# Graph layers: rows through DRAM lines and spreading loads, and score masks added by two DMAs a block

## The reference

```python
for l in range(3):
    si = x @ attn_w[l, :d]
    sj = x @ attn_w[l, d:]
    scores = si[:, :, None] + sj[:, None, :] + attn_b[l]
    scores = jnp.where(scores >= 0, scores, 0.2 * scores)
    scores = jnp.where(mask, scores, -jnp.inf)
    attn = jax.nn.softmax(scores, axis=-1)
    agg = jnp.einsum('bij,bjd->bid', attn, x)
    h = layernorm(x + agg, g1[l], beta1[l])
    ff = jax.nn.gelu(h @ W1[l] + b1[l], approximate=False) @ W2[l] + b2[l]
    x = layernorm(h + ff, g2[l], beta2[l])
```

## Time and profile before

| | |
|---|---|
| time, median of 3 runs | 2490.27 us (2487.1 to 2490.76) |
| the profiled execution's own time | 2482.05 us |
| its span in the trace | 2480.2 us |
| block with `v_row` (odd k), first two layers | 37.3 us |
| block without `v_row` (even k), first two layers | 36.3 us |
| ten blocks of the last layer (34 to 43) | 377.2 us |
| TensorE clock granted, mean of the execution | 0.974 |

### The profile page before, as it was taken

The page is one execution under the profiler, slowest core; times in us unless marked ns, Lnnn a source line. Parts: engine busy times, 40 slices in busy tenths (PEclk is TensorE's granted clock), DMA queues, the critical chain, the costliest instruction groups (busy, mean ns, idle before and its releaser), DMA issues. The chain is left out here.

```text
span 2480.2 us, 45887 instructions
## 1 busy us (share of the span) xinstructions
PE 2361.1 (95%) x16548; PEld 2187.9 (88%) x16548; DVE 2072.0 (84%) x4806; ACT 1784.7 (72%) x2849; POOL 1122.7 (45%) x1317
## 2 busy tenths in 40 slices
PE   7999999993599999999999999999999999999996
PEld 6999999982499999999999999999999999999996
DVE  5888888885678998988878898998887989889875
ACT  3444445442478888888878889888887888888883
POOL 3555555563233353453434353354443555544531
PEclk9999999996699999999999999999999999999998
DMA  4444444444646657755666757656666566566441
GB/s 149 136 139 139 145 146 139 143 124 111 176 117 151 175 138 174 182 144 144 156 169 163 168 143 179 169 138 158 162 160 166 147 162 158 140 170 133 116 110 43
DMA packets 382131, 364.78 MB, mean 147 GB/s; under 512 B 218064, under 2 KB 312272, under 8 KB 381904
## 3 DMA queue, kind: packets, MB, share of 16 engines
q1 hardware_dynamic: 354256, 261.17, 38.5%
q0 software_dynamic: 27648, 100.68, 17.3%
HBM read 152.07 MB, written 58.72 MB: 85 GB/s over the span
## 5 line engine op out<-in xcount | busy, mean ns | idle before, releaser
L1490 PE MATMUL A<-x_hi,pT_hi 128*128 128x258 f32 x1536 | 439.4, 286 | 28.5 <-DVE pT_lo L1233 21.7
L1144 ACT ACTIVATE g<-G,b_less 128x512 f32<-128x512 f32 x384 | 264.4, 688 | 261.7 <-PE G L45 260.1
L1491 PE MATMUL A<-x_hi,pT_lo 128*128 128x258 f32 x1536 | 437.1, 285 | 0.0
L1492 PE MATMUL A<-x_lo,pT_hi 128*128 128x256 f32 x1536 | 434.3, 283 | 0.0
L1541 PE MATMUL Y<-w,g_hi 128*128 128x256 f32 x1536 | 433.0, 282 | 0.0
L1542 PE MATMUL Y<-w,g_hi 128*128 128x256 f32 x1536 | 427.0, 278 | 0.0
L1543 PE MATMUL Y<-w,g_lo 128*128 128x256 f32 x1536 | 426.6, 278 | 0.0
L1049 POOL DMA_DIRECT2D t<-maskT x192 | 173.4, 955 | 403.6 <-DVE t L1226 398.5
L1233 DVE TENSOR_TENSOR pT_lo<-t,pT_hi 128x512 fp32r<-128x512 f32 x384 | 259.0, 687 | 103.7 <-ACT t L1109 103.4
L1322 DVE TENSOR_TENSOR g_lo<-g,g_hi 128x512 fp32r<-128x512 f32 x384 | 264.2, 688 | 93.5 <-ACT g_hi L1147 90.1
L1490 PEld LDWEIGHTS A<-x_hi,pT_hi 128*128 128x128 f32 x1536 | 293.2, 191 | 37.9 <-issue 22.6
(11 more groups left out here) (184 smaller groups left out, 6082.1 us busy)
## 6 DMA issues: line engine op xcount, KB each, us to landing
t<-maskT POOLq DMA_DIRECT2D x192, 512.0 KB, 4.7
mask<-mask SPq DMA_DIRECT2D x192, 256.0 KB, 2.9
a_adj_t<-in_adj SPq DMA_DIRECT2D x64, 512.0 KB, 4.0
x_rows<-rows SPq DMA_DIRECT2D x24, 1024.0 KB, 6.6
mask<-a_mask SPq DMA_DIRECT2D x64, 256.0 KB, 4.3
rows<-xo SPq DMA_DIRECT2D x32, 512.0 KB, 2.9
a_xs<-in_x SPq DMA_DIRECT2D x9, 1024.0 KB, 9.6
x_rows<-in_x SPq DMA_DIRECT2D x8, 1024.0 KB, 7.2
```

Of the source, the lines that this page charges most:

```text
L1490: pe.matmul(L.A[:, t, 0:DE], hi, L.x_hi[:, par, j, :], start=(j == 0), stop=False)
L1491: pe.matmul(L.A[:, t, 0:DE], lo, L.x_hi[:, par, j, :], start=False, stop=False)
L1492: mm = pe.matmul(L.A[:, t, 0:D], hi, L.x_lo[:, par, j, :], start=False, stop=(j == NT - 1))
```

## The change

1. **Rows.** For blocks 2 to 47 PE makes one small transpose per graph instead of the eight: `r_line` (rcol, 128 by 16, to 16 by 128) at f = 2 of even blocks, and `v_line` (vcol, 128 by 8, to 8 by 128) at f = 1 of odd blocks. ACT copies the result to a small SBUF tile, SP stores it as a line in DRAM, and SP loads that line back into all 128 partitions (`partition_broadcast`). 21 such lines for vrow, 23 for rrow; each rrow line is read by four loads of 256 KB, each vrow line by one of 512 KB. The first three v rows and the first two r rows are made as before.
2. **Masks.** `add_masks` issues two DMAs of four tiles (semaphores tm0 and tm1) in place of four of two. The first needs score tile 3 and now stands behind `deviation1`; the second needs score tile 7 and stands behind `deviation3`. `exps` of tiles 4 and 5 therefore now waits for the DMA that needs score tile 7.

```diff
@@ masks, SP and POOL
                 if k > 0:
-                    for g in range(2 * half, 2 * half + 2):
-                        sp.wait_ge(L.s_tm[g], 16 * k)
+                    sp.wait_ge(L.s_tm[half], 16 * k)
...
             def add_masks(k, groups):
                 for g in groups:
-                    pool.wait_ge(L.s_t, NT * k + 2 * g + 2)
-                    pool.wait_ge(L.s_maskT[g // 2], 16 * (k + 1))
-                    pool.dma_start(L.t[:, 2 * g:2 * g + 2, :], L.maskT[:, 2 * g:2 * g + 2, :], accum_op=ALU.add).then_inc(L.s_tm[g], 16)
+                    gs = slice(HALF * g, HALF * (g + 1))
+                    pool.wait_ge(L.s_t, NT * k + HALF * (g + 1))
+                    pool.wait_ge(L.s_maskT[g], 16 * (k + 1))
+                    pool.dma_start(L.t[:, gs, :], L.maskT[:, gs, :], accum_op=ALU.add).then_inc(L.s_tm[g], 16)
@@ ACT, exps
-                act.wait_ge(L.s_tm[j // 2], 16 * (k + 1))
+                act.wait_ge(L.s_tm[j // HALF], 16 * (k + 1))
@@ SP, rows
+            def store_v(n):
+                sp.wait_ge(L.s_vline, n - PB + 1)
+                sp.dma_start(vline[n].rearrange("(s p) -> s p", p=P), L.v_line[:, :]).then_inc(L.s_vline_out, 16)
+
+            def load_v(n):
+                sp.wait_ge(L.s_vline_out, 16 * (n - PB + 1))
+                sp.wait_ge(L.s_top, NT * (n - 1))
+                sp.dma_start(L.vrow[:, n % 2, :], vline[n].partition_broadcast(P)).then_inc(L.s_vrow_in[n % 2], 16)
...
+            def load_r(k):
+                n, cs = k // 2, slice(k % 2 * BANK, (k % 2 + 1) * BANK)
+                sp.wait_ge(L.s_rline_out, 16 * n)
+                sp.wait_ge(L.s_t, NT * (k - 1))
+                for part in range(2):
+                    sp.dma_start(L.rrow[:, part, k % 2, :], rline[n, part, cs].partition_broadcast(P)).then_inc(L.s_rrow_in[k % 2], 16)
@@ PE, rows
+            def v_line(n):
+
+                pe.wait_ge(L.s_vprep, 4 * n + 1)
+                pe.transpose(L.A[0:NT, 2, 0:P], L.vcol[:, :], L.ident[:, :]).then_inc(L.s_vlineT, 1)
+
+            def r_line(n):
+
+                pe.wait_ge(L.s_cols, COLS * (n + 1))
+                pe.transpose(L.A[0:2 * NT, 0, 0:P], L.rcol[:, :, :].rearrange("p a s -> p (a s)"), L.ident[:, :]).then_inc(L.s_rlineT, 1)
```

More of the change, by code:

```diff
@@ L732, in layer_buffers @@
     L.s_vrow = sem("vrow")
+    L.s_vlineT = sem("vlineT")
+    L.s_vline = sem("vline")
+    L.s_vline_out = sem("vline_out")
+    L.s_vrow_in = [sem(f"vrow_in{i}") for i in range(2)]
     L.s_top = sem("top")
@@ L736, in layer_buffers @@
     L.s_rrow = sem("rrow")
+    L.s_rlineT = sem("rlineT")
+    L.s_rline = sem("rline")
+    L.s_rline_out = sem("rline_out")
+    L.s_rrow_in = [sem(f"rrow_in{i}") for i in range(2)]
     L.s_t = sem("t")
-    L.s_tm = [sem(f"tm{i}") for i in range(4)]
+    L.s_tm = [sem(f"tm{i}") for i in range(2)]
     L.s_exp = sem("exp")
@@ L770, in layer_buffers, with graph_layers @@
     return L
-def graph_layers(nc, L, x, rows, out, mask, split, par):
+def graph_layers(nc, L, x, rows, out, mask, split, vline, rline, par):
     attn_w, attn_b, W1, b1, W2, b2, g1, be1, g2, be2 = par
@@ L927, in _ @@
                     load_x1(k - 2)
+                if k % 2 == 1 and k + 2 < K:
+                    load_r(k + 2)
                 for f in split_at(k):
@@ L942, in _ @@
                     load_maskT(k + 2, 0)
+                for n in r_made(k):
+                    store_r(n)
+                for n in v_made(k):
+                    if n >= PB:
+                        store_v(n)
                 for f in split_at(k):
@@ L947, in _ @@
                         load_split(arriving, f)
+                for n in v_made(k):
+                    if n >= PB:
+                        load_v(n)
+                for n in r_made(k):
+                    load_r(2 * n)
                 for r in tops[2:]:
@@ L1054, in _ @@
             v_prepare(1)
-            add_masks(0, range(4))
+            add_masks(0, range(2))
             for k in range(K + 2):
@@ L1061, in _ @@
                         row_columns((k + 2) // 2, part)
-                for n in rows_made(k):
+                for n in v_made(k):
                     v_prepare(n)
-                if k + 1 < K:
-                    add_masks(k + 1, range(1))
                 if k < K:
@@ L1068, in _ @@
                 if k + 1 < K:
-                    add_masks(k + 1, range(1, 3))
+                    add_masks(k + 1, range(1))
                 if k - 2 >= K - C:
@@ L1072, in _ @@
                 if k + 1 < K:
-                    add_masks(k + 1, range(3, 4))
+                    add_masks(k + 1, range(1, 2))
         @block.scalar
@@ L1089, in copy_v, with copy_v_line, copy_r_line @@
                 act.activation(L.vrow[:, n % 2, :].rearrange("p (c i) -> p c i", c=2), L.A[:, 2:4, :], ACT.Copy).then_inc(L.s_vrow, 1)
+            def copy_v_line(n):
+                act.wait_ge(L.s_vlineT, n - PB + 1)
+                if n > PB:
+                    act.wait_ge(L.s_vline_out, 16 * (n - PB))
+                act.activation(L.v_line[:, :], L.A[0:NT, 2, 0:P], ACT.Copy).then_inc(L.s_vline, 1)
+            def copy_r_line(n):
+                act.wait_ge(L.s_rlineT, n)
+                if n >= 2:
+                    act.wait_ge(L.s_rline_out, 16 * (n - 1))
+                act.activation(L.r_line[:, :], L.A[0:2 * NT, 0, 0:P], ACT.Copy).then_inc(L.s_rline, 1)
             def x_hi(j):
@@ L1184, in _ @@
                     if f == 3:
-                        for n in rows_made(k):
-                            copy_v(n)
-                    if f == 4 and k + 2 < K:
-                        for part in range(2):
-                            copy_rows(k + 2, part)
+                        for n in v_made(k):
+                            if n < PB:
+                                copy_v(n)
+                            else:
+                                copy_v_line(n)
+                        for n in r_made(k):
+                            copy_r_line(n)
                     if f in (5, 6) and k < K:
@@ L1568, in _ @@
                         pe.wait_ge(L.s_u, TC * (k + 1))
-                        for n in rows_made(k):
-                            v_row(n)
-                    if f == 2 and k + 2 < K:
-                        r_rows(k + 2)
+                        for n in v_made(k):
+                            if n < PB:
+                                v_row(n)
+                            else:
+                                v_line(n)
+                    if f == 2:
+                        for n in r_made(k):
+                            r_line(n)
                     if ffn:
@@ L1585, in program @@
     split = nc.dram_tensor("split", (layers - 1, W1.shape[2] // P, P, 4, D), F32, kind="Internal").ap()
+    vline = nc.dram_tensor("vline", (layers * B, N), F32, kind="Internal").ap()
+    rline = nc.dram_tensor("rline", (layers * B, 2, N), F32, kind="Internal").ap()
     chunks = rows.rearrange("(c t) p d -> c p t d", t=TC)
@@ L1594, in program @@
         L = layer_buffers(nc, ctx, x, W1, x_rows, s_rows, uv)
[L1595 removed]
+        graph_layers(nc, L, x, chunks, out_chunks, mask, split, vline, rline, par)
 _INS = ['x', 'adj', 'L0_gnn_W', 'L0_gnn_b', 'L0_gnn_attn', 'L1_gnn_attn_w', 'L1_gnn_attn_b', 'L1_gnn_W1', 'L1_gnn_b1',
```

43 lines of the change are left out of this document (32 added, 11 removed).

## The result

The changed kernel takes 2542.67 us (median of 4 runs, 2531.89 to 2558.45) against 2490.11 us for the kernel before (now 4 runs): a ratio of 1.0218, 95% interval 1.0184 to 1.0251, or +52.6 us. The prediction said slower, by 25 us. Half of the loss was missing in it.

A forecast was written before the change was run, and what follows sets the result against it. PE was taken to bound the first two layers, with DVE and ACT close. Terms -1 (first layers), +20 (last layer), +2, +2, +2 summed to +25 us: 2515 us on the median of 2490.27, range 2454 to 2550.

The forecast's parts named there:

- PE sets the time in the first two layers; rows are worth 53 us of PE.: First two layers: PE bounds the blocks; rows take net 53 us off PE, blocks come to some 35.6 us.
- Landing L of a four-tile addition: Mask additions: time from issue to landing of four tiles, 6.1 us undisturbed, 8.0 us taken.
- The collision in the first layers: Transposing load of maskT's first half meets the second four-tile addition and puts about 2 us on its landing.
- the loop: First two layers: a block takes 29.1 + L, or 28.5 + L without a weight slice; -1 us in all.
- the rival "cancel": Gain and loss cancel: L = 7.0, first layers -29, last +10, 2480 to 2495 us; chance 0.13.
- The rival of an undisturbed addition: PE's gain kept: L stays 6.1, PE sets 35.65 us a block in the first layers, 2458 us; chance 0.28.
- The last layer's loop, 31.7 + L: Last layer, second addition behind `deviation3`: 39.7 us a block, 397 for ten against 377.2, +20 us.
- The new loads are far from their users ... I cost them at nothing.: Row lines' store and load land by 30 us, first read some 33 us after the same start; cost nothing.
- The two changes of layer ... +1 each.: Changes of layer: weight loads stand in SP's queue behind the wait for tm1, +1 us each.
- Smaller terms: Blocks 44 to 46 +2 us, first block +2, the two changes of layer +1 each.
- Much slower: Weight stores also hit the addition, L from 9, 2557 us, perhaps lost clock; chance 0.13 together with late rows.

The follow-up runs named there:

- rows_tuned2: Rows of the change on the kernel before, masks as before; last-layer store, weights and mask rows moved ahead of the line in SP's queue: 2452.09 us.
- held: Changed kernel, but the transposing load of maskT's first half waits for both mask additions: 2590.18 us.
- masks_only: Kernel before with only the mask part of the change, two four-tile additions in their new places: 2517.23 us.
- after: Profiled execution of the changed kernel, against the kernel before, the longest of its four runs: 2558.45 us.
- line_last: Changed kernel with the lines' stores and loads moved to the end of SP's turn: 2513.11 us.
- rows alone: Kernel before with only the row part of the change, masks still added by four two-tile DMAs: 2474.66 us.
- both moves: Changed kernel, last-layer store ahead of maskT's first half and new weights' loads ahead of the line in SP's queue: 2501.76 us.
- the weights' move: Kernel before with all new weights' loads issued right behind the transposing load of maskT's first half: 2487.02 us.
- early_store: Changed kernel with the last layer's store issued ahead of maskT's first half in SP's queue: 2511.68 us.
- forced_plus: `masks_forced` with one small write to a new scratch tile on POOL ahead of the last layer's second addition: 2530.77 us.
- masks_forced: `masks_only`, but in the last layer maskT's first-half load waits for the end of rstd2, which also releases the second addition: 2524.83 us.

## Why the prediction was right and wrong

1. *PE sets the time in the first two layers; rows are worth 53 us of PE.* Right in kind, and 10 us too large. Blocks without a slice came to 35.5 to 36.3 us (35.65 forecast), and in `rows_tuned2` PE is 43.6 us less busy. In the change itself it is 13 us, not 50, less busy, with a granted clock of 0.96 over the whole against 0.974.
2. *Landing L of a four-tile addition.* 6.1 undisturbed was near: 5.7 to 6.3 in `held`. The collision in the first layers was sized too large: L = 7.03 on average in blocks without a slice and 7.5 in those with one, not 8.0. With 28.5 + 7.03 = 35.5 the loop stays under PE's 35.65, with 29.1 + 7.5 = 36.6 it doesn't (37.2 measured). Hence -8.9 instead of -1. In L this part went the way of the rival "cancel" (L = 7.0), in time only a part of its way (-29). The rival of an undisturbed addition did not come: in ordinary blocks it took over 1 us more than the 5.8 us when alone. The prediction had drawn that rival from what the Trainium skill, "DMA: Bandwidth & Descriptors", section on queues, rings and completion order, says of engines that go round their queues packet by packet; the trace agrees with the slower addition and not with the undisturbed one, and whether the engines go round so is not shown by it.
3. *The last layer's loop, 31.7 + L.* Right as a mechanism, and close in size: `masks_only` has L = 7.42 on average in blocks 35 to 43, which makes 39.1, and its blocks took 39.0. In the change, L = 9.03 makes 40.7, and 16.9 us of waiting for the store in ten blocks make 42.4, against 42.3 measured. The term was 20 and measured 45.7: some 10 us of the difference by the larger L, which holds the late landings of this execution, and 17 by the store.
4. *"The new loads are far from their users ... I cost them at nothing."* This is the step that failed. The loads did land in time: DVE never waited for them in after. But their round trip is a wait in the middle of an in-order queue, and I counted only who reads the rows, not who stands behind the wait. Those are the new weights, the store of the last layer and maskT's second half. What stood there at nothing measured 26 us of the 52.6: that is what `line_last` took off by moving only the round trip. Moving those who stood behind it instead took off 25 us (the store) and 19 us (the weights), 44 together.
5. *"The two changes of layer ... +1 each."* The same failure: +25.5 in the profiled executions. Weight loads behind tm1 were seen, the line ahead of them not. Masks alone made blocks 17 and 18 7 us longer, rows alone 9.5, both 19.4, of which block 18's long landing is some 10 in that execution.
6. *Smaller terms.* First blocks +5.4 for +2; blocks 44 to 47 +8.4 for +2, with the last layer's causes.
7. *"Much slower", decided by L = 9 from the weights' stores, with a loss of clock.* Its time, 2557, is near that of the profiled execution, the longest of four, but by another way: the last layer's L did come to 9.0, the first layers' did not. The loss of granted clock did come, 0.84 in blocks 17 and 33 (0.92 and 0.89 before) and 0.96 in the last layer (1.00 before).

The measured 2542.67 us lies in the stated range, 2454 to 2550, and on the side that was forecast. The side is not mere luck: the masks alone cost 32.7 us, 13 of them in the ten last-layer blocks by the loop that was forecast. That the range held is partly luck. With both moves, which take away what the sum had left out, the changed kernel stands at +8.3 us and not at +25: the rest of the sum was some 17 us too high (6.5 of them are the weights' move, which the kernel before would gain too), and that hid a part of the missing 44.

## What to carry to other kernels

A line that is stored to DRAM and loaded back has two prices: when its reader wants it, and what stands behind the wait for its store on the queue that issues it; list every instruction behind that wait before costing it at nothing. Put such round trips behind whatever others wait for, but not so far that the reader waits (34 us of DVE's time in `line_last`), and look for stores that hold a buffer. A larger DMA in place of two small ones makes the first half as late as the second: add the landing to the loop it stands in, and check it against what sets the time in each stage.

## What the runs showed of the hardware

An accumulating DMA of 1 MB within SBUF lands in 5.7 to 5.8 us when alone (`held`), of 0.5 MB in 3.9. Issued 1.3 us ahead of a transposing load it landed in 7.0 us, time after time. The distance at issue does not settle it: issued 1.9 us ahead it landed in 6.0 us in the last layer of `early_store`, but in 7.0 us in the first two layers of the change (blocks 17, 20 and 24). In the stretches below, as in the earlier trace rows, a transposing load whose packets come first takes the engines whole, and the addition takes them whole behind it. By queue in after (packets, MB, share of 16 engines): block 37, 2053.0 to 2054.5 us; block 38, 2102.0 to 2104.5; block 37 again, 2059.0 to 2062.0:

```profile
q1 hardware_dynamic: 1208, 0.31, 110.3%
...
q0 software_dynamic: 87, 0.71, 104.2%
q1 hardware_dynamic: 7, 0.00, 0.4%
...
q0 software_dynamic: 35, 0.27, 35.6%
q1 hardware_dynamic: 35, 0.01, 1.8%
```

The last stretch is the tail of a long landing: the addition's packets take a third of the engines' time and more than half of it stands idle. Single packets of 8 KB, 0.48 us as a rule, took up to 4.8 us in that landing.

In `forced_plus`, which adds a scratch tile of 64 bytes a partition and a write to it in the last layer alone, most blocks of the first two layers took 36.6 and 37.5 to 37.6 us (even and odd); in `masks_only` they took 36.4 and 37.2. Against `masks_forced`, from which it differs by this tile and write, that makes 2.5 us in 30 blocks. The two ran on different chips, and whether the tile is the cause is not shown.
